# Softmax attention on one core: a second buffer for the maxima, and the small instructions between them

## The reference

```python
# 16 heads of 8, S = 2048
scores = jnp.einsum('bhqe,bhke->bhqk', q, k) * scale
attn = jax.nn.softmax(scores, axis=-1)
out = jnp.einsum('bhqk,bhke->bhqe', attn, v)
```

## Time and profile before

| | us |
|---|---|
| median of 3 runs | 1807.25 |
| lowest, highest | 1806.93, 1807.55 |
| profiled execution | 1806.73 |
| its span, first to last instruction | 1805.0 |

### The profile page before, as it was taken

One profiled execution on the slowest core, in us unless ns is written; L12 is line 12 of the kernel. 1 busy time (PEld: TensorE's weight loads), 2 busy tenths in 40 slices (PEclk: granted clock), 3 DMA queues, 4 the chain that ended last, 5 costly groups with the idle time before them and its releaser, 6 DMA issues. The chain is left out here.

```text
span 1805.0 us, 21953 instructions
## 1 busy us (share of the span) xinstructions
PE 1551.2 (86%) x7396; PEld 638.6 (35%) x7408; DVE 1325.5 (73%) x1954; ACT 860.4 (48%) x1502; POOL 222.5 (12%) x145
## 2 busy tenths in 40 slices
PE   6987348999999999999998889899994566689999
PEld 3433201222222222222223434366663332366665
DVE  5775576898989889988871777656655899655554
ACT  2442314778777788778787434322223000232221
POOL 2222130000000000000000132211101344201110
PEclk8998659999999999999999999899996787799999
DMA  6000230001100110011000000000000000000000
GB/s 173 5 0 1 84 78 15 14 26 42 31 15 26 42 31 14 27 43 31 2 2 1 1 0 0 1 0 1 0 1 0 0 1 0 1 1 6 6 6 7
DMA packets 35618, 33.11 MB, mean 18 GB/s; under 512 B 7452, under 2 KB 30792, under 8 KB 35528
## 3 DMA queue, kind: packets, MB, share of 16 engines
q1 hardware_dynamic: 35528, 31.98, 6.8%
HBM read 25.80 MB, written 4.19 MB: 17 GB/s over the span
## 5 line engine op out<-in xcount | busy, mean ns | idle before, releaser
L1394 DVE TENSOR_REDUCE mx<-ps 128x2 f32<-128x1024 f32 x512 | 600.2, 1220 | 97.4 <-PE ps L1294 96.9
L1381 ACT ACTIVATE xT<-ps 128x512 f32<-128x512 f32 x512 | 289.8, 595 | 118.0 <-PE ps L1322 114.5
L1381 ACT ACTIVATE xn<-ps 128x512 f32<-128x512 f32 x512 | 287.3, 598 | 58.4 <-PE ps L1322 56.7
L1322 PE MATMUL ps<-q,k 84*128 84x512 bf16 x1024 | 308.7, 385 | 2.8 <-DMA q<-neg_turned 1.5
L1294 PE MATMUL ps<-k,q 64*128 64x512 bf16 x1024 | 180.2, 413 | 74.0 <-DVE mx L1394 42.9
L858 ACT ACTIVATE silu<-ps 128x512 f32<-128x512 f32 x144 | 85.3, 596 | 265.2 <-PE ps L831 261.9
L1322 PEld LDWEIGHTS ps<-q,k 84*128 84x128 bf16 x1024 | 62.1, 97 | 290.2 <-ACT xT L1381 135.9
L893 DVE TENSOR_TENSOR hid<-ps,silu 128x512 f32<-128x512 f32 x144 | 97.7, 689 | 90.0 <-PE ps L835 88.2
L831 PE MATMUL ps<-xT,ew 128*128 (+1 forms) x288 | 150.4, 604 | 6.4 <-PEq L1825 4.8
L821 PEld LDWEIGHTS ps<-ew,hid 128*128 128x128 f32 x1152 | 138.7, 192 | 30.6 <-issue 29.9
L835 PE MATMUL ps<-xT,ew 128*128 (+1 forms) x288 | 148.9, 599 | 0.0
(11 more groups left out here) (246 smaller groups left out, 1661.9 us busy)
## 6 DMA issues: line engine op xcount, KB each, us to landing
k<-k_parts SPq DMA_DIRECT2D x84, 64.0 KB
q<-q_parts SPq DMA_DIRECT2D x144, 32.0 KB
q<-q_parts SPq DMA_DIRECT2D x128, 24.0 KB
k<-k_parts SPq DMA_DIRECT2D x24, 96.0 KB
ew<-in_L_ffn_w_dram SPq DMA_DIRECT2D x2, 1024.0 KB
wraw<-in_L_ffn_w_dram SPq DMA_DIRECT2D x3, 512.0 KB, 6.7
q_parts<-part SPq DMA_DIRECT2D x4, 384.0 KB, 4.3
k_parts<-part SPq DMA_DIRECT2D x4, 384.0 KB, 3.0
```

The source lines that it names most:

```text
L1322: nc.tensor.matmul(m.ps[:, BANK[n], :], k2[:, h, kt * P:(kt + 1) * P], q[:, qc, h, :], start=True, stop=True).then_inc(s2_ready, 1)
L1381: nc.scalar.activation(ex[kt % P_RING][:, h, :], m.ps[:, BANK[n], :], ACT.Exp)\
L1394: nc.vector.reduce_max(both, m.ps[:, 2 * (i % 2):2 * (i % 2) + 2, :], AX.X)\
```

## The change

`mx`, the buffer of the maxima, gets a second copy, used by odd units. The seven small instructions become a function `pack(u, k)`. They don't stand behind a unit's own 32 maxima any more but between the first five maxima of the unit behind it, as `PACK_IN` says: k = 0 behind the first, 1 and 2 behind the second, 3 behind the third, 4 and 5 behind the fourth, the transposition behind the fifth. Units 0 and 15 are packed in one go, at once. `HOLE` is gone, so that every slot has one pair, and `LEAD` is 10: in slots 0 to 21 there are pairs of unit u + 1, from slot 22 on those of unit u + 2, and in unit 0 the 32 pairs of unit 1 are in the first 22 slots.

```diff
--- before.py
+++ after.py
@@ -36,8 +36,7 @@
 TILE_1 = 64
 PR = GH // 2
 VC = HD + 1
-LEAD = 8
-HOLE = 1
+LEAD = 10
 WARM = 6
 PART_RING = 4
 P_RING = 2
@@ -1126,7 +1125,7 @@
 
         ex = [m.xT[:, :].rearrange("p (h t) -> p h t", t=CHUNK),
               m.xn[:, :, :].rearrange("p (h a) d -> p h (a d)", a=TPC)]
-        mx = m.sb("mx", [P, GH, TPC, CHUNKS], stack=stack)
+        mx = m.sb("mx", [P, 2, GH, TPC, CHUNKS], stack=stack)
         neg = m.sb("neg", [P, GH, TPC], stack=stack)
         neg_rest = m.sb("neg_rest", [P, 2, GH, TPC], stack=stack)
 
@@ -1134,8 +1133,7 @@
         S1B, S2B, AVB = [0, 1, 2, 3], [4, 5, 6], 7
 
         SLOTS = 2 * TILES
-        done = [max(0, (k + 1 - HOLE) * PAIRS // (SLOTS - HOLE)) for k in range(-1, SLOTS)]
-        S1_IN = [range(done[k], done[k + 1]) for k in range(SLOTS)]
+        S1_IN = [range(k * PAIRS // SLOTS, (k + 1) * PAIRS // SLOTS) for k in range(SLOTS)]
         EARLY = [range(k * PAIRS // (SLOTS - LEAD), (k + 1) * PAIRS // (SLOTS - LEAD)) for k in range(SLOTS - LEAD)]
 
 
@@ -1143,6 +1141,7 @@
         WIDE = S2B + S1B
         BANK = [S2B[n % len(S2B)] for n in range(LAST)] + [WIDE[n % len(WIDE)] for n in range(STEPS)]
         USED_BY = [next((k for k in range(n - 1, -1, -1) if BANK[k] == BANK[n]), None) for n in range(UNITS * STEPS)]
+        PACK_IN = [(0,), (1, 2), (3,), (4, 5), (6,)]
         block = stack.enter_context(nc.Block())
 
 
@@ -1386,38 +1385,55 @@
 
         @block.vector
         def _(dve):
-            def maxima(u, first=False):
+            out = neg_part[:, :, 0:PARTS * GH].rearrange("p t (i h) -> p h t i", h=GH)
+
+            def pack(u, k):
+
+                if k == 0:
+                    dve.wait_ge(s1_used, (u + 1) * PAIRS)
+                    nc.vector.tensor_reduce(neg[:, :, :], mx[:, u % 2, :, :, :], axis=AX.X, op=ALU.max, negate=True)\
+                        .then_inc(max_steps, 1)
+                    return
+                dve.wait_ge(max_steps, u * 6 + k)
+                if k == 1:
+                    nc.vector.tensor_copy(out[:, :, :, 0], neg[:, :, :]).then_inc(max_steps, 1)
+                elif k == 2:
+                    nc.vector.tensor_tensor(neg_rest[:, 0, :, :], neg[:, :, :], out[:, :, :, 0], ALU.subtract)\
+                        .then_inc(max_steps, 1)
+                elif k == 3:
+                    nc.vector.tensor_copy(out[:, :, :, 1], neg_rest[:, 0, :, :]).then_inc(max_steps, 1)
+                elif k == 4:
+                    nc.vector.tensor_tensor(neg_rest[:, 1, :, :], neg_rest[:, 0, :, :], out[:, :, :, 1], ALU.subtract)\
+                        .then_inc(max_steps, 1)
+                elif k == 5:
+                    nc.vector.tensor_copy(out[:, :, :, 2], neg_rest[:, 1, :, :]).then_inc(max_steps, 1)
+                else:
+                    if u > 0:
+                        dve.wait_ge(max_loaded, DMAS_M * u)
+                    nc.vector.transpose(neg_turned[:, :, :].rearrange("p j t -> p t j"), neg_part[:, :, :])\
+                        .then_inc(max_turned, 1)
+                    dve.wait_ge(max_turned, u + 1)
+
+            def maxima(u, between):
+
                 for i in range(PAIRS):
                     dve.wait_ge(s1_ready, u * PAIRS + (i + 1))
                     pr, qt, kc = i // (TPC * CHUNKS), i // CHUNKS % TPC, i % CHUNKS
-                    both = mx[:, :, qt, kc].rearrange("p (s r) -> p r s", r=PR)[:, pr, :]
+                    both = mx[:, u % 2, :, qt, kc].rearrange("p (s r) -> p r s", r=PR)[:, pr, :]
                     nc.vector.reduce_max(both, m.ps[:, 2 * (i % 2):2 * (i % 2) + 2, :], AX.X)\
                         .then_inc(s1_used, 1)
-                dve.wait_ge(s1_used, (u + 1) * PAIRS)
-
-                nc.vector.tensor_reduce(neg[:, :, :], mx[:, :, :, :], axis=AX.X, op=ALU.max, negate=True)\
-                    .then_inc(max_steps, 1)
-                dve.wait_ge(max_steps, u * 6 + 1)
-                out = neg_part[:, :, 0:PARTS * GH].rearrange("p t (i h) -> p h t i", h=GH)
-                nc.vector.tensor_copy(out[:, :, :, 0], neg[:, :, :]).then_inc(max_steps, 1)
-                dve.wait_ge(max_steps, u * 6 + 2)
-                nc.vector.tensor_tensor(neg_rest[:, 0, :, :], neg[:, :, :], out[:, :, :, 0], ALU.subtract).then_inc(max_steps, 1)
-                dve.wait_ge(max_steps, u * 6 + 3)
-                nc.vector.tensor_copy(out[:, :, :, 1], neg_rest[:, 0, :, :]).then_inc(max_steps, 1)
-                dve.wait_ge(max_steps, u * 6 + 4)
-                nc.vector.tensor_tensor(neg_rest[:, 1, :, :], neg_rest[:, 0, :, :], out[:, :, :, 1], ALU.subtract)\
-                    .then_inc(max_steps, 1)
-                dve.wait_ge(max_steps, u * 6 + 5)
-                nc.vector.tensor_copy(out[:, :, :, 2], neg_rest[:, 1, :, :]).then_inc(max_steps, 1)
-                dve.wait_ge(max_steps, u * 6 + 6)
-                if not first:
-                    dve.wait_ge(max_loaded, DMAS_M * u)
-                nc.vector.transpose(neg_turned[:, :, :].rearrange("p j t -> p t j"), neg_part[:, :, :]).then_inc(max_turned, 1)
-                dve.wait_ge(max_turned, u + 1)
-
-            maxima(0, True)
-            for u in range(1, UNITS):
-                maxima(u)
+                    if between and i < len(PACK_IN):
+                        for k in PACK_IN[i]:
+                            pack(u - 1, k)
+
+            maxima(0, False)
+            for k in range(7):
+                pack(0, k)
+            maxima(1, False)
+            for u in range(2, UNITS):
+                maxima(u, True)
+            for k in range(7):
+                pack(UNITS - 1, k)
 
 
     m.stage()
```

## The result

| | before | after |
|---|---|---|
| median, us | 1807.74 (15 runs, 1805.85 to 1810.34) | 1812.25 (15 runs, 1808.17 to 1816.66) |
| profiled execution, us | 1806.73 | 1813.64 |

The ratio is 1.0022 with a 95% interval of 1.0015 to 1.0030: the changed kernel is slower, by 2.7 to 5.4 us, and the medians lie 4.5 us apart. The forecast was 6.7 slower.

A forecast was written before the change was run, and what follows sets the result against it. TensorE was taken to bound the kernel, with VectorE's maxima close behind. Unit 0 +4.8, units 1 to 13 +3.6 and unit 14 -1.74 summed to +6.7 us: 1813.9 us, 0.4% slower, range 1807 to 1821.

The forecast's parts named there:

- What bounds: Softmax stage: TensorE is busiest, 622 of 648 us; VectorE has slack of 0.25 us a step but almost no depth.
- The walk of steps 11 to 14: Where small instructions are spread: TensorE stalls 0.12, 0.10 and 0.50 us behind late maxima; transposition ends at 7.55.
- The load: At a unit's start: first score 4.60 us after the transposition, so TensorE waits another 1.22 us for the maxima's load.
- The unit: Units 1 to 13: excess over regular steps 1.95 us against 1.67, +0.28 us a unit, +3.6 in all.
- Unit 0: Ten three-pair steps instead of eight +3.0 us, two steps becoming regular -0.19, new excess +1.95: sum +4.8.
- Unit 14: No pairs from slot 22 on: its 4.12 us step becomes one without pairs, 2.38, so -1.74 us.
- What is behind the moved load: SyncE's queue, every fourth unit: six k1 loads, landing 1.2 us after issue, have 6.6 us to spare and stay hidden.
- The hidden load (1): Rival: path from transposition to first score under 3.4 us, load hidden, -0.95 us a unit, 1796.7 us; chance 0.12.
- All of the excess going (2): Rival: spreading the small instructions is free too, 1.67 us a unit saved, 1786.6 us; chance 0.03.
- No overlap (3): Rival: VectorE's small instructions don't overlap their neighbours, excess 2.26 us a unit, 1818.3 us; chance 0.15.
- The clock (4): Rival: TensorE's clock falls behind each of 14 waits, up to 2.5 us each, 35 us, 1849 us; chance 0.03.
- The price of an issue: SyncE's queue after the transposition: four loads of neg_turned take 3.3 us to issue, 0.83 each.

## Why the prediction was right, and where it was off

- *What bounds.* Right. The steps of 2.61 and 2.65 us stand in both traces, and VectorE's lateness of 0.05 to 0.13 us is paid at once.
- *The walk of steps 11 to 14.* Right in each place, and in sum a little high. Forecast stalls 0.12, 0.10, 0.50; measured 549.49 - 546.73 - 2.63 = 0.13, 552.17 - 549.49 - 2.63 = 0.05, and 552.87 - 552.17 - 0.25 = 0.45. The transposition's end was forecast at 7.55, and is at 551.55 - 544.12 = 7.43 (A's matmuls being 0.44 ahead of 544.56).
- *The load.* Right: 4.51 to 4.61 in units 1 to 14, and with leads of 8 and 9 it is the same, while two queues shorten it to 3.40 or less. The wait is 1.00 and not 1.22.
- *The unit.* +0.28 forecast, +0.17 measured, the sum of both points above. From unit 1's first score to unit 14's it is 570.3 against 568.4, +2.0 where 3.6 were forecast. This is the term that was mis-sized: a difference of two excesses, 1.67 and 1.95, of which the second measured 1.84, so an error of a tenth of a us moves the result by a third.
- *Unit 0.* Ten long steps and the wait of 1.0, as said. Yet between the first scores of units 0 and 1 there are only 2.2 us more, not 4.8, because the profiled execution of before has its first steps at a low clock and the one of after has not. The window from 279 to 300 us, columns as in the earlier trace rows, before:

```profile
279.00:300.00 21.00, 17.89 (x90) 3.19 (x91) 15.18 (x13) 11.83 (x23) 0.00 (x0) 0.84 0.08 21
```

And after:

```profile
279.00:300.00 21.00, 16.32 (x95) 3.48 (x97) 16.32 (x14) 12.35 (x24) 0.00 (x0) 1.00 0.08 26
```

  The first two steps have the same pairs in both kernels. From unit 0's first score (before: 277.75) to the pairs of its third step, before:

```profile
288.92 0.63 PE L1294 MATMUL ps<-k,q 64*128 64x512 bf16 x4
```

  And after:

```profile
278.99 0.82 PE L1321 MATMUL ps<-q,k 84*128 84x512 bf16 x3 [0.36 <-DMA q<-neg_turned]
...
287.61 0.62 PE L1293 MATMUL ps<-k,q 64*128 64x512 bf16 x4
```

  That is 11.17 us before and 8.62 after, 2.55 less; with that put back unit 0 costs 4.7. The profile of before, taken as the base, hid this; the forecast used full-clock rows for the term and so had it right.
- *Unit 14.* -1.74 forecast, -1.73 measured (42.79 to 41.06 between first scores).
- *Second mx buffer.* Nothing, 0.21 us as before.
- *What is behind the moved load.* The conclusion held, the step did not. The prediction let k1's loads land 1.2 us after their issue, as the maxima's do. With the lead of 11 they take 6.7 to 7.5, so of the 6.6 us to spare 0.3 to 1.0 were there. One slot more of lead moves the pair that reads them from the start of a step to the second place of the one before, 2.4 us earlier, and that is more.
- *The sum.* 2.2 + 2.0 - 1.7 = 2.5, the stage's own difference. With 2.55 put back for the clock in unit 0 the stage costs 5.0, near the 4.5 between the medians. The forecast's +6.7 was right in sign and cause and about 2 too high, 1.6 of it from the units. That the profiled pair differs by 6.9, almost the forecast, is luck: 4.3 of it lies outside the stage.
- *Rivals.* The hidden load (1) is out. All of the excess going (2) is out. No overlap (3) is out: each small instruction starts or is followed with 0.08 to 0.13 of overlap wherever nothing is waited for (545.70 + 0.21 against 545.83). The section of the Trainium skill that the prediction set beside this rival ("VectorE: DVE Perf Modes", section "The DRAIN you can't avoid") has the next operation start when the pipe is empty, but adds that one that isn't held starts earlier. That is what the small instructions of this trace do. The clock (4) didn't fall in the changed kernel's units 0 to 14, but it does behind waits of 2.65.
- *The price of an issue.* Right: 3.30 us for four on SyncE's queue, 0.83 each. On GpSimd's queue it is 0.54.
Open: why the first steps of unit 0 are at half clock in some profiled executions (before, and both with a lead of 11, down to a mean of 0.59 from 279 to 300 us) and not in others. The wait for the load just ahead of them doesn't sort them: it was 1.46, 0.78 and 0.61 us in these three, and 0.69 and 0.65 in two that kept the clock (the lead of 9, and the small instructions one maximum earlier). The low clock accounts for the rest of the lead of 11's distance from its expectation as far as the one execution shows, and what it is in the other runs was not seen.

## What to carry to other kernels

When work is spread out to fill holes, look at what hangs on its last piece: here the last piece started a path of 4.6 us that had 1.4 to spare, and it was moved towards the first score by more than that. The same seven instructions one maximum earlier are 14 us faster. Cost the path as issues in a row on one queue plus a landing, since splitting it over two queues shortens it, and count the loads queued behind it with their own landing time.

A wait that repeats can have a second price, a fall of the clock behind it. Here it came behind waits of 2.65 us and not behind 1.00, and behind 2.65 not every time, so read the granted clock behind each wait of a design.

## What the runs showed of the hardware

- Behind one wait of 1.00 us TensorE's clock stayed at 2.4 GHz in 14 of 14 unit starts. Behind 2.65 us it fell to 1.2 GHz in 10 of 14, behind 4.10 in 14 of 14. Behind two waits of 0.71 and 0.72 us, a pair apart, it fell in 5 of 13 units, though together they are 1.43. A fall cost about 1.5 us with two short waits and 1.5 to 2.9 behind 2.65.
- Issuing one of these loads of 12 KB takes 0.83 us of SyncE's queue and 0.54 of GpSimd's, and the two queues work side by side.
- The pair that waits for six k1 loads of 64 to 96 KB starts 6.7 to 7.5 us after the last is issued, the score that waits for four maxima loads of 12 KB 1.2 us after.
- VectorE's maxima start 1.13 to 1.14 us apart where nothing is waited for, though each lasts 1.22 to 1.23. In unit 0 with the third pair later thirty of them are busy for 34.9 us and idle for 0.9, 1.19 apart on average.
